# Normalising the rows of two attentions on ScalarE instead of VectorE

## The reference, cut to what matters

```python
def _layernorm(x, axis=-1, eps=1e-05):
    m = jnp.mean(x, axis=axis, keepdims=True)
    v = jnp.var(x, axis=axis, keepdims=True)
    return (x - m) / jnp.sqrt(v + eps)
```

## Time and profile before

| | us |
|---|---|
| median of 3 runs | 640.24 |
| the profiled execution | 638.77 |
| its span, first to last instruction | 637.0 |
| mean granted TensorE clock, share of full | 0.91 |
| VectorE busy, share of the span | 388.7, 61% |
| ScalarE busy | 259.4, 41% |
| GpSimd busy | 256.8, 40% |
| TensorE busy (matmuls) | 525.2, 82% |

### The profile page before, as it was taken

How to read it: one execution, slowest core, us unless ns; L and a number is a source line. 1 busy time by engine, 2 the same in 40 slices (tenths; PEclk the granted TensorE clock), 3 DMA queues, 4 the chain that set the end, 5 groups by cost and what they waited for, 6 DMA issues and landing times.

```text
span 637.0 us, 10302 instructions
## 1 busy us (share of the span) xinstructions
PE 525.2 (82%) x3381; PEld 391.6 (61%) x3382; DVE 388.7 (61%) x782; ACT 259.4 (41%) x441; POOL 256.8 (40%) x321
## 2 busy tenths in 40 slices
PE   5957798888787568999999999958588888577994
PEld 2433574745576358999999999954244355343653
DVE  4277878777845654433243322216588998958993
ACT  1133643455273124344344423220343545435884
POOL 3453424223420072111111101017346667737996
PEclk9976999998989559999999999995899999787999
DMA  6920010010006506480644410003000000000001
GB/s 206 295 107 1 0 34 2 0 34 0 21 14 221 208 16 210 162 304 21 230 151 132 177 33 28 13 26 99 25 0 1 1 2 1 1 0 1 33 33 67
DMA packets 28631, 46.36 MB, mean 73 GB/s; under 512 B 2381, under 2 KB 24921, under 8 KB 26553
## 3 DMA queue, kind: packets, MB, share of 16 engines
q1 hardware_dynamic: 24328, 39.02, 18.2%
q0 software_dynamic: 1680, 4.59, 2.4%
q10 hardware_dynamic: 2592, 2.36, 1.1%
HBM read 38.36 MB, written 7.60 MB: 72 GB/s over the span
## 4 chain that ended last, share of the span: by engine, by line
PE 51%; DVE 28%; issue 6%; ACT 6%; POOL 5%; DMA 2%; DVEq 0%; SPq 0%; ACTq 0%; POOLq 0%
PE bank L890 19%; PE bank L902 8%; DVE s_max L1329 4%; DVE p_sum L1347 4%; DVE probs L1337 4%; PE bank L656 4%; PE bank L754 3%; PE bank L764 3%; PE bank L968 2%; ACT probs L1035 2%; DVE ew L1288 2%; PE bank L667 2%; DVE stats L1266 2%; DVE xn L1288 2%; PE bank L812 1%
## 5 line engine op out<-in xcount | busy, mean ns | idle before, releaser
L890 PE MATMUL bank<-q_t,ew 128*128 128x128 f32 x1152 | 137.9, 279 | 0.9 <-ACT q_t L1148 0.5
L890 PEld LDWEIGHTS bank<-q_t,ew 128*128 128x128 f32 x1152 | 133.9, 195 | 2.7 <-DVE probs_t L1598 1.6
L463 POOL TENSOR_TENSOR probs<-probs,p_rcp 128x1024 f32<-128x1024 f32 x32 | 61.9, 1936 | 120.6 <-DVE p_rcp L1350 120.6
L1598 DVE TENSOR_TENSOR probs_t<-bank,probs 128x512 f32<-128x512 f32 x36 | 24.8, 690 | 78.3 <-ACT probs L1154 78.3
L667 PE MATMUL bank<-k_bd,q_t 128*128 128x512 f32 x128 | 65.1, 628 | 3.5 <-ACT q_t L1030 3.5
L1035 ACT ACTIVATE probs<-probs 128x1024 f32<-128x1024 f32 x32 | 33.9, 1058 | 60.5 <-DVE probs L1337 60.5
L523 POOL TENSOR_TENSOR token_now<-token_of,carried 128x1 uint32<-128x1 uint32 x17 | 6.6, 387 | 127.4 <-PE bank L876 127.4
L681 PE MATMUL bank<-ident,probs 128*128 128x128 f32 x256 | 37.5, 294 | 21.4 <-POOL probs L463 20.5
L681 PEld LDWEIGHTS bank<-ident,probs 128*128 128x128 f32 x256 | 31.4, 151 | 38.6 <-POOL probs L463 28.5
L1065 ACT COPY probs_t<-bank 128x512 f32<-128x512 f32 x64 | 34.7, 592 | 49.9 <-PE bank L681 49.8
L1329 DVE TENSOR_REDUCE s_max<-bank 128x8 f32<-128x512 f32 x64 | 40.5, 674 | 21.2 <-PE bank L667 21.1
(11 more groups left out here) (206 smaller groups left out, 1091.3 us busy)
## 6 DMA issues: line engine op xcount, KB each, us to landing
ew<-in_L_ffn_w SPq DMA_DIRECT2D x8, 2048.0 KB
ew<-in_L_ffn_w SPq DMA_DIRECT2D x8, 1024.0 KB, 5.8
slots_y<-xn ACTq DMA_DIRECT2D x18, 128.0 KB, 1.9
x_res<-in_x SPq DMA_DIRECT2D x4, 512.0 KB, 6.8
token_rows<-ew SPq DMA_DIRECT2D x4, 512.0 KB, 3.0
out_rows<-x_res SPq DMA_DIRECT2D x3, 512.0 KB, 2.9
w<-in_L_xattn_W SPq DMA_DIRECT2D x2, 512.0 KB, 8.6
ew<-in_L_ffn_w_gate SPq DMA_DIRECT2D x1, 1024.0 KB, 8.8
```

Source lines behind the costliest of these rows:

```text
L463: nc.gpsimd.tensor_tensor(p, p, p_rcp[:, i, :].unsqueeze(2).to_broadcast([P, H, M]), ALU.mult).then_inc(s["p_norm"], 1)
L890: last = nc.tensor.matmul(o[:, P * j:P * j + P], ew1[:, s, k, c0:c0 + P], xs_t[:, par, k, :], start=(k == 0), stop=(k == DK - 1))
```

## The change

In ten places (counted in the order of execution) four instructions of VectorE go and four of ScalarE come. These are the `l0` rows of batches 2 and 3 (and a third time, without use, of the rows behind the last batch), the `rt` rows of all four batches, and the `ff` rows of batches 0, 1 and 2. ScalarE makes `rstd * x + neg_shift` with both factors read from one value per row. The first two batches of `l0` and `l1` and the last of `ff` keep VectorE's form. GpSimd makes two more small products in every normalisation: `neg_mean` ahead of the power and `neg_shift` behind it. The count of the semaphore `rstd` doubles, and some waits are added that keep `mv`, `rstd` and `neg_shift` until they are read.

```diff
-        def layer_norm_rstd(pool, s, n, tiles=slice(0, TB)):
+        def layer_norm_rstd(pool, s, n, used=None):
+            if used is not None:
+                pool.wait_ge(*used)
             pool.wait_ge(s["aggr"], n)
...
+            nc.gpsimd.tensor_tensor(var_eps[:], mv[:, :, 1], eps[:], ALU.add).then_inc(s["eps"], 1)
+            nc.gpsimd.tensor_tensor(neg_mean[:], mv[:, :, 0], minus_one[:], ALU.mult).then_inc(s["eps"], 1)
+            pool.wait_ge(s["eps"], 2 * n)
+            nc.gpsimd.tensor_tensor(rstd[:], var_eps[:], minus_half[:], ALU.pow).then_inc(s["rstd"], 1)
+            pool.wait_ge(s["rstd"], 2 * n - 1)
+            nc.gpsimd.tensor_tensor(neg_shift[:], neg_mean[:], rstd[:], ALU.mult).then_inc(s["rstd"], 1)
...
@@ gpsimd, batch(l, b, first, last)
+                second = ln["rt" if l == 0 else "ff"]
                 if not last:
-                    layer_norm_rstd(pool, ln["l0" if l == 0 else "l1"], b + 3)
+                    layer_norm_rstd(pool, ln["l0" if l == 0 else "l1"], b + 3, (ln["l0" if l == 0 else "l1"]["rstd"], 4) if first else (second["xn"], b))
...
@@ scalar
+            def norm_rows(ph, n, t0, out):
+                act.wait_ge(ln[ph]["rstd"], 2 * n)
+                for i in range(TB):
+                    last = nc.scalar.activation(out[:, i, :], x_res[:, bass.ds(t0 + i, 1), :].rearrange("p o d -> p (o d)"),
+                                                ACT.Identity, bias=neg_shift[:, i:i + 1], scale=rstd[:, i:i + 1])
+                last.then_inc(ln[ph]["xn"], 1)
+
+            def routed_rows(b):
+                act.wait_ge(d_rows, 16 * b)
+                norm_rows("rt", b + 1, TB * b, xn2)
...
                 turned(0)
                 turned(1)
                 if l == 0 and not first_batch:
+                    routed_rows(b - 1)
                     router_rows(b - 1)
+                if l == 1 and not first_batch:
+                    norm_rows("ff", b, TB * b - TB, xn2)
                 exps(l, b, 2)
                 output(0, 0)
...
                 output(1, 1)
+                if l == 0 and not last_batch:
+                    act.wait_ge(s["t_xt"], DK * b + 2 * DK)
+                    norm_rows("l0", b + 3, TB * b + 2 * TB, xn)
...
             attention(0, B - 1, False, True)
+            routed_rows(B - 1)
             router_rows(B - 1)
...
@@ vector
-            def join_stats(s, n):
+            def join_stats(s, n, used=None):
+                if used is not None:
+                    dve.wait_ge(*used)
...
-                if l == 1 and not (first_batch or last_batch):
-                    norm_apply(second, b, TB * b - TB, xn2)
                 sums(l, b, 2)
...
                 if not last_batch:
-                    join_stats(phase, b + 3)
-                if l == 1 and last_batch:
-                    norm_apply(second, b, TB * b - TB, xn2)
+                    join_stats(phase, b + 3, None if first_batch else (second["eps"], 2 * b))
                 if l == 1 and not first_batch:
                     row_scales(b - 1)
                 if not last_batch:
                     scores(l, b + 1, 0)
-                    if l == 0:
-                        dve.wait_ge(s["t_xt"], DK * b + 2 * DK)
-                        norm_apply(phase, b + 3, TB * b + 2 * TB, xn)
                     sums(l, b + 1, 0)
...
-                    norm_stats(second, b + 1, TB * b)
-                if l == 0:
-                    if not first_batch:
-                        dve.wait_ge(d_rows, 16 * b)
-                    norm_apply(second, b + 1, TB * b, xn2)
+                    norm_stats(second, b + 1, TB * b, (phase["eps"], 2 * b + 6))
```

More of the change, by code:

```diff
@@ L73, in flamingo @@
         minus_half = sb("minus_half", [P, TB])
+        minus_one = sb("minus_one", [P, TB])
         eps = sb("eps", [P, TB])
@@ L97, in flamingo @@
         rstd = sb("rstd", [P, TB])
+        neg_mean = sb("neg_mean", [P, TB])
+        neg_shift = sb("neg_shift", [P, TB])
         ctx_rows = sb("ctx_rows", [P, 2, C])
@@ L363, in _ @@
             sp.wait_ge(d_out, 16 * (B + 1))
-        def layer_norm_rstd(pool, s, n, tiles=slice(0, TB)):
+        def layer_norm_rstd(pool, s, n, used=None):
+            if used is not None:
+                pool.wait_ge(*used)
             pool.wait_ge(s["aggr"], n)
-            nc.gpsimd.tensor_tensor(var_eps[:, tiles], mv[:, tiles, 1], eps[:, tiles], ALU.add).then_inc(s["eps"], 1)
-            pool.wait_ge(s["eps"], n)
-            nc.gpsimd.tensor_tensor(rstd[:, tiles], var_eps[:, tiles], minus_half[:, tiles], ALU.pow).then_inc(s["rstd"], 1)
+            nc.gpsimd.tensor_tensor(var_eps[:], mv[:, :, 1], eps[:], ALU.add).then_inc(s["eps"], 1)
[4 more added lines that the diff above has]
+            nc.gpsimd.tensor_tensor(neg_shift[:], neg_mean[:], rstd[:], ALU.mult).then_inc(s["rstd"], 1)
         @block.gpsimd
@@ L380, in _ @@
             nc.gpsimd.memset(minus_half[:], -0.5).then_inc(p_const, 1)
+            nc.gpsimd.memset(minus_one[:], -1.0).then_inc(p_const, 1)
             nc.gpsimd.memset(carried[:, 2:3], 0.0).then_inc(p_const, 1)
@@ L472, in scale_rows @@
             def scale_rows(b):
-                pool.wait_ge(ln["l1"]["rstd"], b + 1)
+                pool.wait_ge(ln["l1"]["rstd"], 2 * b + 1)
                 pool.wait_ge(p_xm, b - 1)
@@ L500, in batch @@
                         ternary(b)
-                layer_norm_rstd(pool, ln["rt" if l == 0 else "ff"], b + 1)
+                if last:
+                    layer_norm_rstd(pool, second, b + 1, (second["xn"], b))
+                else:
+                    layer_norm_rstd(pool, second, b + 1, (ln["l0"]["xn"], b + 3) if l == 0 else (ln["l1"]["rstd"], 2 * b + 6))
             normalise(0, 0, 0)
             normalise(0, 0, 1)
-            layer_norm_rstd(pool, ln["l0"], 2)
+            layer_norm_rstd(pool, ln["l0"], 2, (ln["l0"]["rstd"], 2))
             pool.wait_ge(p_wlo, 2)
@@ L559, in _ @@
                 if g >= 2:
-                    layer_norm_rstd(pool, ln["l1"], g - 1)
+                    layer_norm_rstd(pool, ln["l1"], g - 1, (ln["rt"]["xn"], B) if g == 2 else (ln["l1"]["rstd"], 2))
             normalise(1, 0, 0)
@@ L603, in _ @@
         def _(pe):
-            pe.wait_ge(p_const, 20)
+            pe.wait_ge(p_const, 21)
             pe.wait_ge(d_vec, 16 * 5)
@@ L1276, in join_stats, with norm_stats @@
                 last.then_inc(s["aggr"], 1)
-            def norm_stats(s, n, t0):
+            def norm_stats(s, n, t0, used=None):
                 carry_wait()
                 row_stats(s, t0)
-                join_stats(s, n)
+                join_stats(s, n, used)
             def norm_apply(s, n, t0, out):
                 dve.wait_ge(s["aggr"], n)
-                dve.wait_ge(s["rstd"], n)
+                dve.wait_ge(s["rstd"], 2 * n - 1)
                 for i in range(TB):
@@ L1480, in attention @@
                 if last_batch:
-                    join_stats(second, b + 1)
+                    join_stats(second, b + 1, (second["eps"], 2 * b))
                 else:
-                    norm_stats(second, b + 1, TB * b)
-                if l == 0:
-                    if not first_batch:
-                        dve.wait_ge(d_rows, 16 * b)
-                    norm_apply(second, b + 1, TB * b, xn2)
+                    norm_stats(second, b + 1, TB * b, (phase["eps"], 2 * b + 6))
             attention(0, 0, True, False)
@@ L1629, in _ @@
                 row_stats(ln["l1"], 0, GATHERS[g])
-            join_stats(ln["l1"], 1)
+            join_stats(ln["l1"], 1, (ln["rt"]["eps"], 2 * B))
             norm_apply(ln["l1"], 1, 0, xn)
```

6 lines of the change are left out of this document (3 added, 3 removed).

## The result

The changed kernel has a median of 642.7 us (639.54 to 645.43, 20 runs), the kernel before, beside it, 640.51 us (639.22 to 642.47, 20 runs). The ratio is 1.0032, with a 95% interval of 1.0019 to 1.0045: slower by 2.2 us or 0.3%, just at what a measurement of this kernel can tell. The forecast was 644.3 us (640.5 to 648.0) with 0.74 on "slower". A second set of runs gave 644.02 us and 1.0043 [1.002, 1.0065].

The account below looks back on a forecast made before the run. The prediction saw layer 1's attention chain as nearly all VectorE, layer 0's as alternating between TensorE, VectorE and ScalarE. Layer 0 at 0.0 plus layer 1 at +4.1 us gave 644.3 us, range 640.5 to 648.0.

Parts of the forecast that it names:

- layer 0: `rt` and `l0` rows and prelude: gains and losses were to sum to 0.0 us.
- layer 1: `ff` rows ahead of the exponential of tile 2: +2.0 us in batches 1 and 2, +0.1 in batch 3, sum +4.1.
- Four instructions: ScalarE's four new applying instructions, overlapping, were to take 2.0 us in each place.
- `l0` -0.4, -0.76, -0.76: Layer 0, `l0` rows: the sum starts earlier without VectorE's four, -0.4 us in batch 0, -0.8 in batches 1 and 2.
- after the last batch: Layer 0, `rt` rows of the last batch, alone on the chain: +1.1 us.
- batch 3 of layer 1: Exponential of tile 2 delayed by 2.3 us, `ff_rows` about 1 us earlier, gain lost at the next wait: +0.1 us.
- the second factor is free: Rival, all places: four instructions take 1.6 us instead of 2.0, sum +1.3, 641.5 us; chance 0.15.
- Batch 3: ... 3.30 against 0.45 + 2.0: -0.8: Layer 0, `rt` rows: GpSimd's `bias_rows` held VectorE's four to 3.30 us, ScalarE isn't held: -0.8 us.
- a rival with a chance of 0.10: Layer 0: shorter gaps keep TensorE's clock up in three half-speed stretches, -2.1 us in all, 638.1 us; chance 0.10.
- Batch 1: ... without a gap worth naming, so +1.1: Layer 0, `rt` rows: TensorE's list up to the second half of `queries` had no gap to absorb the delay: +1.1 us.
- VectorE gets its work back: Rival, layer 1: exponential not held by the new four, 1.4 us gained twice, something in batch 3, about 636; chance 0.03.
- VectorE's busy time: Whole kernel: VectorE was to be busy about 19 us less while the span grows.

Follow-up runs that it names:

- only_ff: The kernel before with only the `ff` rows moved to ScalarE, ahead of the exponential of tile 2: 646.58 us, ratio to before 1.0086.
- ff_behind: The changed kernel with the `ff` rows still on ScalarE but behind the exponential in its list: 639.56 us, ratio to before 0.9982.
- ff_on_dve: The changed kernel with the `ff` rows back on VectorE, `l0` and `rt` staying on ScalarE: 640.95 us, ratio to before 1.0012.
- after_third: The changed kernel, unchanged, run a third time for its profile: one time, 645.68 us.
- after_again: The changed kernel, unchanged, run once more for a second profile: 644.02 us, ratio to before 1.0043.

## Why the prediction was right, and where it was not

**The sign and its cause were right.** The forecast was 0.0 for layer 0 and +4.1 for layer 1. Layer 1 measured +4.3, +3.4 and +4.6 us in the three profiles of the changed kernel (sum of the last stages up to `gate`), and undoing its order alone gave back 4.5 us, undoing its move 3.1 us (with intervals that overlap), in medians. The parts by themselves give -1.2 (l0), -1.5 (rt) and +6.0 (ff), together +3.3, where the whole gave +2.2 and +3.5.

**Most of its small terms held.** Four instructions 2.07 us (2.0 forecast); GpSimd 0.48 (0.45); +2.3 and +2.0 to +2.2 a batch (+2.0); `l0` -0.4, -0.76, -0.76 (-0.4, -0.8, -0.8); after the last batch +1.1 (+1.1); batch 3 of layer 1 0.0, -1.1 and +0.1 (+0.1), where the exponential of tile 2 came 2.3 us later in its stage (10.12 us after that of tile 1, against 7.84) and the later waits made up for it. That the second factor is free is excluded (0.589 us).

**The mis-sized step: "Batch 3: ... 3.30 against 0.45 + 2.0: -0.8".** This term of layer 0 measured -2.7 in all seven profiles that have it. The mechanism named was right, but two more stood beside it. Before, then the changed kernel, behind the powers at 168.69 (in both):

```profile
174.38 1.29 DVE L1337 TENSOR_TENSOR probs<-bank,s_max 128x512 f32<-128x512 f32 x2
175.70 1.06 ACT L1035 ACTIVATE probs<-probs 128x1024 f32<-128x1024 f32 x1 [0.67 <-DVE probs L1337]
```

```profile
173.93 1.07 ACT L1048 ACTIVATE probs<-probs 128x1024 f32<-128x1024 f32 x1
```

- The transposes start at 172.31 instead of 173.29: -1.0. This is the term as forecast (-0.8).
- The exponential of tile 2 starts at 173.93 instead of 175.70, another -0.8. Before, it waited for a subtraction of VectorE that stood behind the four. The prediction had put such freedom of VectorE at nothing. That held after batch 0, where ScalarE itself was late by about as much (5.28 us from power to exponential against 5.18), but not here, where ScalarE is early. It is a term left out, not the clock.
- The other -1.0 comes behind that exponential, where before has the half-speed stretch that I had seen (0.57 from 174 to 182) and had left to a rival with a chance of 0.10 that needed "nearly all three" stretches to go. In all seven profiles with these rows on VectorE such a stretch begins 5 to 15 us behind the power; in the seven others none does within 30 us. So it went for sure with the move, and belonged in the sum. Why it goes is argued only. The wait of TensorE ahead of the transposes is 2.38 to 2.52 us in the one group and 1.56 to 1.69 in the other, but a stretch also begins behind a wait of 1.95 us (at 108.55 in the changed kernel), so the length of one wait doesn't decide it.

**A second term, "Batch 1: ... without a gap worth naming, so +1.1",** measured +0.1: from the power to the exponential of tile 0 it takes 105.30 - 86.10 = 19.20 us against 105.27 - 86.18 = 19.09. TensorE's list had no gap there because it ran at half speed. Busy time and clock from 93 to 96 us, before and then the changed kernel:

```profile
93.00:96.00 3.00, 3.00 (x17) 1.86 (x16) 2.83 (x6) 1.45 (x3) 1.90 (x1) 0.50 0.00 0
```

```profile
93.00:96.00 3.00, 2.84 (x25) 1.95 (x25) 2.83 (x6) 1.41 (x3) 1.90 (x1) 1.00 0.00 0
```

In only_ff, where these rows stay on VectorE and that stretch is absent, the wait shows, and the 1.1 would have fitted into it:

```profile
97.80 1.95 PE L681 MATMUL bank<-xn_t,wq 128*128 128x512 f32 x4 [1.43 <-DVE logits L1425]
```

From rt0 to rt1 the changed kernel measured +1.3 where +1.1 - 0.8 = +0.3 was forecast. The +1.1 isn't in it, and what is instead is a new half-speed stretch, at 120 us, which ff_behind and ff_on_dve, with the same layer 0, don't have. From rt1 to rt2 -1.2 was measured where +0.3 - 0.8 = -0.5 was forecast. The changed kernel has half-speed stretches which before has not, and the reverse (stretches of the timeline: busy and count of the five engines, then the granted clock). The changed kernel:

```profile
110.00:112.00 2.00, 2.00 (x6) 1.53 (x5) 1.02 (x2) 1.23 (x2) 0.00 (x0) 0.50 0.00 0
120.00:123.00 3.00, 3.00 (x16) 3.00 (x16) 2.96 (x4) 0.00 (x0) 0.28 (x1) 0.50 0.00 0
148.00:154.00 6.00, 3.85 (x20) 2.26 (x13) 4.81 (x9) 4.23 (x8) 2.91 (x2) 1.00 0.00 0
170.00:184.00 14.00, 10.03 (x114) 7.79 (x116) 6.98 (x13) 11.30 (x18) 6.10 (x3) 1.00 0.12 39
```

The kernel before:

```profile
120.00:123.00 3.00, 2.34 (x19) 2.34 (x20) 2.97 (x4) 0.00 (x0) 0.06 (x1) 1.00 0.00 0
150.00:154.00 4.00, 3.48 (x9) 2.71 (x10) 2.95 (x6) 0.62 (x1) 1.84 (x1) 0.58 0.00 0
```

The stretch at 110 stays though the gap ahead of it fell from 2.71 us to 1.95; that at 150 went, as did that at 93, and new ones at 120 and at 137 came. Up to the router's last product the changed kernel measured -1.6 us (and -1.4 in after_third, and +1.1 in after_again, where more half-speed time fell ahead of rt0) against 0.0. With layer 1 that makes 4.3 - 1.6 = 2.7, near the first set of runs (+2.2). The second set (+3.5) lies nearer to the forecast, so which part of the miss in the median is layer 0 stays open.

**The rival "VectorE gets its work back" was mispriced.** It was given 1.4 us twice and 636 us. Its order, ff_behind, measured 639.56: the four of VectorE stood in the shadow of the exponential and were worth 0.28 us. The row that says so was in the prediction: exponential to 494.97, sum at 495.19.

**VectorE's busy time** fell by 15.3 us, not by 19. The applying instructions did fall as forecast, from 32.0 us (L1288) to 12.5 (L1321). Other groups of VectorE rose by 4.2 together, among them the scaling of `x_abs` (L1395, 1.5 to 2.4 us) and `h_lo` (L1416, 14.5 to 15.1); why they rose stays open.

## What to carry over

Where an instruction moves to an engine with an in-order list, its price is set by what stands behind it there: the same four instructions of 2.07 us cost 2 us a batch ahead of the exponential on which the longest chain hangs, and between -0.1 and +0.5 behind it. Freed time counts only as far as the next instruction of the relieved engine could start earlier, so look first at what that one waits for. And choose moves instance by instance: of the router's four groups of rows the last cost 1.1 us every time, while the third, where the four took VectorE 3.30 us beside GpSimd's work and both TensorE and the next exponential waited for VectorE, paid 2.7, and that one, with the `l0` rows moved and the `ff` rows behind the exponential, gave the version that beats both kernels (632.34 us).
